# Five logit buffers, a second source tile on rounded operands, and GpSimd in the head loop of a graph-attention kernel

## The reference, cut to what matters

```python
h = (x @ W.T).reshape(n, heads, out_ch)              # n = 1250, heads = 8, out_ch = 128
a_src = jnp.einsum('nhc,hc->nh', h, att_src)
a_dst = jnp.einsum('nhc,hc->nh', h, att_dst)
e = jax.nn.leaky_relu(a_src[src] + a_dst[dst], 0.2)
m = jax.ops.segment_max(e, dst, num_segments=n)
ex = jnp.exp(e - m[dst])
denom = jax.ops.segment_sum(ex, dst, num_segments=n)
out = jax.ops.segment_sum((ex / (denom[dst] + EPS))[:, :, None] * h[src], dst, num_segments=n)
```

## Time and profile before

| | us |
|---|---|
| median of three executions (lowest, highest) | 714.68 (713.36, 715.59) |
| the profiled execution: its own time | 713.25 |
| its span | 711.4 |
| busy in it: TensorE, VectorE, ScalarE, GpSimd | 701.1, 529.0, 420.0, 114.1 |

### The profile page before, as it was taken

How to read it: one execution, slowest core, us unless ns; L and a number is a source line. 1 busy time by engine, 2 the same in 40 slices (tenths; PEclk the granted TensorE clock), 3 DMA queues, 4 the chain that set the end, 5 groups by cost and what they waited for, 6 DMA issues and landing times.

```text
span 711.4 us, 13502 instructions
## 1 busy us (share of the span) xinstructions
PE 701.1 (99%) x4670; PEld 657.9 (92%) x4670; DVE 529.0 (74%) x878; ACT 420.0 (59%) x863; POOL 114.1 (16%) x95
## 2 busy tenths in 40 slices
PE   8899999999999999999999999999999999999997
PEld 6699999889899999999999999999999899999997
DVE  5999888698899999999999664445568752737232
ACT  4665584388688888888888754454443333522202
POOL 2559421000000000000000000000223331222202
PEclk9999999999999999999999999999999999999999
DMA  8727888645314131322310443201881734315102
GB/s 279 223 68 195 262 244 232 174 140 163 95 40 114 31 102 55 94 67 64 102 32 22 109 111 67 62 0 36 247 282 49 222 91 189 100 58 177 44 23 67
DMA packets 53362, 84.10 MB, mean 118 GB/s; under 512 B 15081, under 2 KB 36399, under 8 KB 53312
## 3 DMA queue, kind: packets, MB, share of 16 engines
q1 hardware_dynamic: 47628, 65.69, 32.6%
q10 hardware_dynamic: 4500, 13.82, 6.0%
q0 software_dynamic: 1184, 3.92, 1.9%
HBM read 68.09 MB, written 15.33 MB: 117 GB/s over the span
## 4 chain that ended last, share of the span: by engine, by line
PE 91%; DMA 4%; DVE 3%; issue 0%; POOL 0%; ACT 0%; ACTq 0%; SPq 0%; DVEq 0%
PE bank L1426 22%; PE bank L1571 13%; PE bank L1402 12%; PE bank L1498 12%; PE bank L1298 11%; PE bank L1675 4%; DMA w1n_sb<-in_W 3%; PE bank L1647 3%; PE bank L1213 3%; PE bank L1552 2%; PE bank L1701 1%; DVE x2f L2312 1%; PE bank L1215 1%; PE bank L1228 1%; PE bank L1732 1%; DVE fc_lo L2279 1%
## 5 line engine op out<-in xcount | busy, mean ns | idle before, releaser
L1426 PE MATMUL bank<-PT,h1s 125*128 125x250 f32 x730 | 161.0, 374 | 0.0
L1426 PEld LDWEIGHTS bank<-PT,h1s 125*128 125x128 f32 x730 | 135.3, 190 | 14.4
L2078 DVE SCALAR_TENSOR_TENSOR L<-asb,nadh 125x1250 f32<-125x1250 f32 x80 | 117.9, 1515 | 1.9 <-PE bank L1402 0.9
L2087 DVE CUSTOM_DVE_ANT_0 L<-L,LC 125x1250 f32<-125x1250 f32 x80 | 113.4, 1454 | 0.6 <-DMA LC<-log_count_scratch 0.4
L914 ACT ACTIVATE L<-L,nm 125x1250 f32<-125x1250 f32 x80 | 108.4, 1384 | 2.7 <-DVE nm L2087 1.9
L932 ACT COPY PT<-bank 125x500 f32<-125x500 f32 x165 | 87.4, 613 | 35.9 <-PE bank L1402 35.9
L1402 PE MATMUL bank<-ident,L 125*125 125x125 f32 x800 | 94.2, 273 | 0.0
L1402 PEld LDWEIGHTS bank<-ident,L 125*125 125x125 f32 x800 | 91.2, 189 | 0.9 <-issue 0.4
L1884 DVE TENSOR_TENSOR hotr<-iota,r 125x1500 f16<-125x1500 f16 x50 | 46.5, 931 | 7.8 <-PE bank L1215 4.2
L743 POOL MEMSET pick<- 128x90 f32 x1 | 0.2, 168 | 267.2 <-ACT hT L965 267.2
L1571 PE MATMUL bank<-h_hi,PT_hi 125*125 125x384 f32 x200 | 41.5, 350 | 0.0
(11 more groups left out here) (285 smaller groups left out, 1353.9 us busy)
## 6 DMA issues: line engine op xcount, KB each, us to landing
asb<-src_logit_rows SPq DMA_DIRECT2D x28, 312.5 KB, 3.9
atom_w<-in_atom_inT SPq DMA_DIRECT2D x5, 1152.0 KB, 12.5
atom_w<-in_atom_outT SPq DMA_DIRECT2D x5, 1152.0 KB, 9.4
log_count_scratch<-LCw SPq DMA_DIRECT2D x10, 546.9 KB
LC<-log_count_scratch SPq DMA_DIRECT2D x10, 546.9 KB
LCt<-log_count_scratch SPq DMA_DIRECT2D x10, 546.9 KB
h_scratch<-h1st ACTq DMA_DIRECT2D x10, 448.0 KB
rdT<-reciprocal_scratch SPq DMA_DIRECT2D x8, 500.0 KB, 4.6
```

The costliest lines, as they stand in the source:

```text
L1426: mm = pe.matmul(sums, h1s[q][:, s, :], PT[p][:, s, :], start=(s == 0), stop=(plain and s == NT - 1))
L2078: dve.scalar_tensor_tensor(L[r][:, :], asb[q][0:NP, 1, :], nadh[q][:, t:t + 1], asb[q][0:NP, 0, :], ALU.add, ALU.max).then_inc(stt_done, 1)
L2087: dve.tensor_tensor_reduce(out=L[r][:, :], in0=L[r][:, :], in1=LC[:, t, :], scale=-1.0, scalar=-FLOOR, op0=ALU.add, op1=ALU.min, accum_out ...
```

## The change

- The ring of logit tiles grows from four to five (`RING`). VectorE's steps no longer cover the two tiles of one group: from step 4 on a step covers tiles `2k+1` and `2k+2` (`blocks`), that is the second of group k and the first of group k+1. ScalarE's step becomes: exponential of the first tile, evacuation of the group before, exponential of the second tile.
- Source tiles 0 and 1 are now computed on rounded operands (`PART = 0`), in the same 35 groups. For tile 0 the rest `PT_lo` is made by VectorE as before. For tile 1 ScalarE writes the negated probability next to the rounded one, and GpSimd makes `PT_neg`, the rounded minus the exact one, by two transfers: a plain one of the negated values, and, when it has landed, one of the rounded values that adds in flight (`accum_op`). The last product takes `h1p_neg`, the negated rounded features.
- GpSimd makes the rests of both feature tiles (`h1p_lo`) and `h1p_neg` once in a head; VectorE's L2099 is gone. VectorE's copy of the destination logits (`nadh`, L2069) is gone too.
- The products of `W2` move from steps 6 and 7 to steps 3 and 4 of the first iteration, and the eight loads of `W2T` become one after them.
- The logit rows of a head come in three loads; `rrow` is one small tile, with a wait for its last store (`rden_stored`); the first two loads of reciprocals (`rdA`) now wait for VectorE's last `scalar_tensor_tensor`, since `rdA` shares memory with `asb[1]`. The semaphores of the second layer's banks are merged with those of the first.

The core of the diff:

```diff
-PART = 2
+PIECES = [0, 834, 1667, 2500]
+RING = 5
+PART = 0
+def blocks(k, first):
+    if first and k < 3:
+        return [(2 * k, 2 * k + 1)]
+    if first and k == 3:
+        return [(6,), (7, 8)]
+    if k == 0:
+        return [(0,), (1, 2)]
+    if k == 2 * NG - 1:
+        return [(2 * k + 1,)]
+    return [(2 * k + 1, 2 * k + 2)]
...
+            sp.wait_ge(wattp, 3)
+            sp.dma_start(w2_sb[:, :, 0:D], W2T.rearrange("(k p) n -> p k n", p=128)).then_inc(w2_in, 16)
...
+            def lower_by_sum(hh, kk):
+                n, p = 2 * NG * hh + kk, kk % 2
+                pool.wait_ge(tb_evac, NG * n + (PART // 2 + 1))
+                alone(pool)
+                pool.dma_start(PT_neg[p][:, :].bitcast(F32), PT[p][:, PART + 1, :]).then_inc(raw_moved, 16)
+                pool.wait_ge(raw_moved, 16 * n + (16 - 16 * NG))
+                alone(pool)
+                pool.dma_start(PT_neg[p][:, :].bitcast(F32), PT_hi[p][:, 1, :].bitcast(F32), accum_op=ALU.add
+                               ).then_inc(lower_moved[p], 16)
+                if kk % NG == 0:
+                    q = kk // NG % 2
+                    pool.wait_ge(features_high, 2 * hh + kk // NG)
+                    alone(pool)
+                    pool.tensor_tensor(h1p_lo[q][:, :, :], h1s[q][:, PART:PART + 2, :], h1p_hi[q][:, :, :].bitcast(F32),
+                                       ALU.subtract)
+                    pool.tensor_scalar(h1p_neg[q][:, :], h1p_hi[q][:, 1, :].bitcast(F32), -1.0, None, ALU.mult
+                                       ).then_inc(features_lower, 1)
...
-                        act.copy(PT_hi[(k - lag) % 2][:, :], turned[0:NP, 0:GW])
-                        act.copy(PT[(k - lag) % 2][:, PART + 1, :], turned[0:NP, GW:2 * GW]).then_inc(tb_evac, 1)
+                        act.copy(PT_hi[(k - lag) % 2][:, :, :],
+                                 turned[0:NP, 0:2 * GW].rearrange("p (s n) -> p s n", s=2))
+                        act.activation(PT[(k - lag) % 2][:, PART + 1, :], turned[0:NP, GW:2 * GW], ACT.Copy, scale=-1.0
+                                       ).then_inc(tb_evac, 1)
...
-                    if plain or s != PART:
+                    if plain or s not in (PART, PART + 1):
...
-                    pe.matmul(sums, h1p[q][:, 0, :], PT_hi[p][:, :], start=False, stop=False)
-                    pe.matmul(sums, h1p[q][:, 1, :], PT_hi[p][:, :], start=False, stop=False)
-                    mm = pe.matmul(sums, h1p[q][:, 0, :], PT_lo[p][:, :], start=False, stop=True)
+                    for s in range(2):
+                        pe.matmul(sums, h1p_hi[q][:, s, :], PT_hi[p][:, s, :], start=False, stop=False)
+                        pe.matmul(sums, h1p_lo[q][:, s, :], PT_hi[p][:, s, :], start=False, stop=False)
+                    pe.matmul(sums, h1p_hi[q][:, 0, :], PT_lo[p][:, :], start=False, stop=False)
+                    pe.wait_ge(lower_moved[p], 16 * NG * hh + 16 * ((k - lag) // 2 - (NG // 2 - p)))
+                    mm = pe.matmul(sums, h1p_neg[q][:, :], PT_neg[p][:, :], start=False, stop=True)
```

More of the change, by code:

```diff
@@ L1444, in turn_reciprocals @@
                     pe.wait_ge(rden_rows, m)
-                if first and k == NG + LATE // 2:
+                if first and k == NG:
                     pe.wait_ge(watt_done, 6)
@@ L2072, in logits @@
-                for j in range(2):
-                    r, t = (2 * k + j) % 4, 2 * g + j
-                    if not (first and k < 2):
-                        dve.wait_ge(tb_full, NG * n + -NG)
-                    elif k == 1:
-                        dve.wait_ge(lc_stored[0], TWO * NG)
-                    dve.scalar_tensor_tensor(L[r][:, :], asb[q][0:NP, 1, :], nadh[q][:, t:t + 1], asb[q][0:NP, 0, :],
-                                             ALU.add, ALU.max).then_inc(stt_done, 1)
-                reciprocals(hh, k, first=first)
```

185 lines of the change are left out of this document (98 added, 87 removed).

## The result

The changed kernel takes 716.14 us (median of 22 executions, 714.23 to 718.49), the kernel before 714.43 (22 executions, 712.48 to 716.52). The ratio is 1.0027, 95% interval 1.0017 to 1.0037: slower by 1.7 us, where 3.0 us less were forecast (711.7). The profiled execution took 715.73 us with a span of 713.9.

A forecast was written before the change was run, and what follows sets the result against it. TensorE's issue distances were taken to bound the kernel; -2.7 us from 35 groups and -0.3 us at the end gave -3.0, from a median of 714.68 to 711.7 us (chance 0.55). Range: 710 to 721.

The forecast's parts named there:

- starved heads: Heads where GpSimd gets in only at VectorE's pauses, making features late: 3.2 us of waiting on TensorE each.
- The third rival: Gain eaten by VectorE becoming the bound, a dearer sixth product and wait, or one starved head; 714 us, chance 0.15.
- TensorE's saving: In 35 groups, one fp32 product fewer and three rounded ones more: -0.078 us a group, -2.7 us in all.
- ScalarE: Longer evacuation copies, +0.22 us a group; 57.5 us over ten groups against TensorE's 62.9, so it stays hidden.
- VectorE: Loses the features' rest and nadh copy: 61.2 us in ten groups, below TensorE; not on the path, no gain.
- GpSimd, per group: PT_neg's two transfers, 3.8 us each, ready at T + 9.1 against T + 12.4, T being the group's transposes' start.
- The second rival: PT_neg's two transfers land late beside other loads in 14 groups, 1.1 us each; +15 us, 727, chance 0.08.
- GpSimd, per head: Two feature instructions take 0.9 us, with 5.8 us available; colliding with VectorE costs 0, bound 0.3 us a head.
- The first rival: VectorE's instruction run starves GpSimd's feature instructions in the head loop; 718.1 us with two heads, 734.1 with seven; chance 0.22.
- The start: VectorE waits 2 to 3 us for head 1's rows, but W2's moved products cover TensorE: 0.
- The end: Last reciprocals wait for the first bank's evacuation, one copy earlier: -0.3 us; rdA's new wait costs 0.

The follow-up runs named there:

- e_best: Changed kernel with four repairs: rdT loaded later, last features stored a step earlier, loop reciprocals before tiles 1 and 2, features loaded two groups later; 712.61 us, ratio 0.9980.
- e_onetile: Changed kernel with only source tile 0 rounded, tile 1 by two fp32 products again, no PT_neg or its transfers; 716.91 us, ratio 1.0045.
- e_best_ring4: Changed kernel with four logit buffers, unshifted tiles, old exponential order, rdT loaded later and features loaded two groups later; 712.20 us, ratio 0.9980.
- e_tail: Changed kernel with SyncE loading rdT only after the last group's first PT_neg transfer has landed; 715.58 us, ratio 1.0020.
- e_store: Changed kernel with ScalarE storing the last tile's features one step earlier; 715.20 us, ratio 1.0012.
- e_feat: Changed kernel with SyncE asking for a head's features two groups later; 716.94 us, ratio 1.0038.

## Why the prediction was wrong

The steady group came out as forecast, and three terms put at nothing, the start, VectorE's order at the boundaries and the loads beside the transfers, took more than the saving. The 716.14 us lie in the stated range of 710 to 721, but by luck: its upper part stood for starved heads, and there were none. The third rival named 714, no difference, but for causes that did not occur either (a bound on VectorE, a dearer sixth product, one starved head).

**TensorE's saving: right.** -0.078 us a group was forecast, e_best's middle gives 2.42 / 33 = 0.073, within the bounds of 0.063 to 0.093; the six rounded products stand 0.115 apart, and the wait for `lower_moved` costs nothing when its transfer has landed. e_onetile shows that the gain doesn't come without the rounding of tile 1, and e_best_ring4 that most of it doesn't come without the fifth buffer and its shift.

**ScalarE: right with five buffers.** It stays below TensorE. The text gave the fifth buffer no gain of its own; e_best_ring4 shows 1.9 us of one, 0.06 us a group. With four buffers ScalarE's longer evacuation (the forecast +0.22) and the shorter period move the second exponential of a group up to its transposes, and only the shift takes it out of their way. A sum of busy times (57.5 of 62.9) couldn't show that; the end of one instruction against the start of another would have.

**VectorE: the sum was right and the order was left out.** 61.2 us were forecast for ten groups, and VectorE is not the bound. But the step "it is not on the path" looked at the logits alone. The reciprocals stand in VectorE's program behind what the new `blocks` puts ahead of them, two instructions more in the loop's first step, and TensorE waits for these with its transposes done: 0.2 to 0.5 us at each of three boundaries, 1.1 in all. An edit that reorders an engine's work has to be costed for each of its results that another engine waits for.

**GpSimd, per group: the size right, the case wrong.** "I take 3.8 twice: ready at T + 9.1, 3.3 us early" was on the safe side for most groups: the plain transfer landed after 2.8 us in the median, the adding one after 3.1, and an undisturbed pair was ready at T + 7.8. But the bound, "twice 8.2", was kept for a rival "in about two groups of a head", with a chance of 0.08, and its arrival was a matter of timing and not of chance: where the rows' loads, then the features' or the reciprocals', go out just with one of the two transfers, the pair is late. TensorE waited for that in 2 groups of 35 in after and in up to 5 in the other traces, from under 0.1 to 1.9 us each. The second rival was thus right in its mechanism and place, but it had 14 groups and 15 us where after lost 2.1. The deadline T + 12.4 was about right for 34 groups (12.4 to 12.7 without a wait, 13.0 at the boundaries) and wrong for the last, which has T + 10.5.

**GpSimd, per head: the cost right, the size wrong.** No product waited for the features. But the two instructions took 2.7 to 3.2 us together in after, not 0.9, and were done at T + 8.1 to 10.1, so 1.5 us or more were left before T + 11.6 and not 4.9. One VectorE instruction beside them took up to 2.48 us instead of 1.46, longer by GpSimd's 1.02 us subtraction. The Trainium skill's "SBUF — State Buffer", section "Who interferes with whom", has two such instructions shut each other out through an exclusive lock, and these 1.02 us agree with it. The first rival, starvation by VectorE, to which I gave 0.22, did not occur in any head of any run; the earlier trace rows was the wrong model for instructions in the head loop.

**The start: the step that failed first.** "Asked for earlier it waits 2 to 3 us, tile 9 ... is exponentiated at about 173.5 ... as it is, 0." The wait for the rows at tile 10 was foreseen, and W2's products as its cover; what was missed is that the rows' loads go out 2.2 us later themselves (and the rows come 3.3 later). The fifth buffer has to lie somewhere. It lies on `LCw[1]`, the diff says so in a wait for `lc_stored`, and I costed neither that wait (2.31 us) nor what is queued behind it: VectorE's tile 4, ScalarE's exponentials, the store, SyncE's loads. The forecast of 0 became 1.4 to 2.3 us.

**The end: the term right, its neighbour missing.** The -0.3 us of the reciprocals came, as 0.25: 100.31 to 100.33 us in six traces of five-buffer kernels without a late transfer there, against 100.56. e_onetile has it too, so it isn't the rounding; what the last two groups save by the rounding (0.15 us) doesn't show in the tail, for a reason that stays open. `rdA`'s new wait did cost nothing: the loads go out 0.2 us ahead of group 38's transposes, in before 0.7 behind them. What was left out is what these loads do to the transfers: `rdA`'s hold up the next to last pair and `rdT`'s then the last, 1.3 us net, and e_tail shows that moving `rdT`'s alone takes it away.

Together, from group 0 to the second layer's last transposes: -2.4 (33 groups of the middle) - 0.25 (end) nearly as forecast, then + 2.3 (start), + 1.1 (boundaries), + 0.8 (transfers in the middle) and + 1.3 (tail) give + 2.85, against 505.83 - 503.07 = 2.76 in the traces.

## What to carry to other kernels

A shorter period on the engine that sets the time is the easy half. The other half is each change's edges: where a new buffer's memory was in use, which results lie behind the work that was put ahead, and which loads go out together with a transfer that now has a deadline. Look at the first and last groups and at the loop's boundaries one by one, as 4.7 of the 5.5 us that were lost here were lost there, and work out the deadline again for the last group. Where a transfer has a deadline of some 10 us, its landing beside other loads is the number to use and not the median.

## What the runs showed of the hardware

- GpSimd's transfers between SBUF tiles (122 KB) landed, from the source views of after, 2.8 us after their issue in the median and 5.1 at the most where they were plain, and 3.1 and 6.4 where they added; the long ones stand beside SyncE's loads of 0.6 to 1 MB. The adding ones also took 0.84 us to issue instead of 0.56. The first row below is the plain transfer, the second the adding one.

```profile
DMA to landing us min/median/max: 2.1/2.8/5.1
...
DMA to landing us min/median/max: 3.0/3.1/6.4
```

- The Trainium skill's "DMA: Bandwidth & Descriptors", section "Anatomy of one DMA — SWDGE (gpsimd) path", makes the plain one an estimated 2.3 us; of the 35 in after, 14 landed after 2.1 to 2.3 us, which agrees, and the median of 2.8 doesn't. Its section "SWDGE vs HWDGE vs iDMA" says that an engine takes turns between the queues that feed it, which would fit the long ones; that this is their cause isn't shown.
- GpSimd's subtraction of 256 columns took 1.0 to 1.5 us in after and its multiplication of 128 columns 1.7 to 2.0 beside VectorE; VectorE needed 0.42 and 0.22 for the same.
- A second exponential that ended 0.24 us ahead of the transposes made the first of them 0.07 us longer (e_best_ring4); one that ended 0.34 us ahead did not.
- The granted clock was below 1.00 between 120 and 430 us in two traces only: 0.50 for 3.4 us in e_store's tail and in e_feat's start, both times 0.3 to 0.4 us after the end of a wait of TensorE of 1.8 to 1.9 us. Waits of 1.3 to 1.9 us in other traces had no such sequel, so that the wait brings the lower clock is not shown.
